# Placing a megakernel's statistics and streamed units by VectorE's other work

## What is computed

```
gn(v):  per group of 2 channels: (v - mean) / sqrt(var + 1e-5)
L0(v):  causal mask (lower triangle), depthwise 6x11 convolution, causal mask again
L1(v):  v + bias[channel, row - column]    (bias from a small three-layer MLP)
x = x + L0(gn(x))
x = x + L1(gn(x))
```

## Time and profile before

| | |
|---|---|
| median of three runs | 2722.15 us (2718.95 to 2722.83) |
| the profiled execution's own time | 2720.33 us |
| its span, first to last instruction | 2718.5 us |
| mean granted TensorE clock | 0.905 |
| VectorE busy | 2307.3 us, 85% |
| TensorE busy | 1986.9 us, 73% |
| ScalarE busy | 1661.5 us, 61% |
| GpSimd busy | 1247.5 us, 46% |
| moved by DMA | 901.17 MB, mean 331 GB/s |

### The profile page before, as it was taken

One profiled execution on the slowest core, in us unless ns is written; L12 is line 12 of the kernel. 1 busy time (PEld: TensorE's weight loads), 2 busy tenths in 40 slices (PEclk: granted clock), 3 DMA queues, 4 the chain that ended last, 5 costly groups with the idle time before them and its releaser, 6 DMA issues. The chain is left out here.

```text
span 2718.5 us, 76785 instructions
## 1 busy us (share of the span) xinstructions
PE 1986.9 (73%) x28880; PEld 1885.9 (69%) x28880; DVE 2307.3 (85%) x4175; ACT 1661.5 (61%) x3051; POOL 1247.5 (46%) x1988
## 2 busy tenths in 40 slices
PE   4299978777787878877678777877768777989500
PEld 0199978777777767877678777777768777879400
DVE  7799988898889988899788998899888996969825
ACT  2177766756576656766567665666657665777521
POOL 1133254545445355544555455454544535655533
PEclk9999999998899989999889988999989998999855
DMA  9756569998899988999799998999889996979899
GB/s 338 274 197 201 192 216 408 357 374 313 325 409 353 367 326 339 399 348 359 293 394 384 353 353 303 405 365 371 323 330 401 354 358 222 351 269 344 303 337 347
DMA packets 316250, 901.17 MB, mean 331 GB/s; under 512 B 42416, under 2 KB 42416, under 8 KB 314000
## 3 DMA queue, kind: packets, MB, share of 16 engines
q1 hardware_dynamic: 199648, 579.79, 58.6%
q10 hardware_dynamic: 116416, 319.37, 30.6%
HBM read 579.50 MB, written 319.68 MB: 331 GB/s over the span
## 5 line engine op out<-in xcount | busy, mean ns | idle before, releaser
L1131 PEld LDWEIGHTS psY<-wsplit,XT 128*128 128x128 f16 x25920 | 1612.4, 102 | 313.7 <-DVE XT L751 116.5
L1131 PE MATMUL psY<-wsplit,XT 128*128 128x168 f16 (+5 forms) x25920 | 1638.1, 223 | 252.5 <-DVE XT L751 217.0
L611 ACT CAST XT<-psT 128x512 f16<-128x512 f32 x720 | 414.5, 576 | 534.6 <-PE psT L1117 316.4
L751 DVE TENSOR_TENSOR XT<-psT,XT 128x512 f16<-128x512 f32 x720 | 493.3, 685 | 191.8 <-ACT XT L611 190.0
L1031 POOL TENSOR_TENSOR xn<-xn,mask 128x512 f32<-128x512 f32 x336 | 440.6, 1311 | 423.4 <-ACT xn L599 364.4
L1117 PE MATMUL psT<-ident,xn 128*128 128x128 f32 x2880 | 486.9, 294 | 177.1 <-POOL xn L1031 136.7
L1066 POOL TENSOR_TENSOR ubuf<-ubuf,bias 128x1024 f32<-128x1024 f32 x184 | 413.5, 2248 | 375.6 <-ACT ubuf L658 375.1
L1057 POOL COPY halo<-XT 128x16 f16<-128x16 f16 x720 | 300.9, 418 | 611.9 <-DVE XT L751 598.9
L779 DVE BATCH_NORM_STATS2 entries<-abuf 128x6 f32<-128x512 f32 x872 | 549.0, 678 | 29.1 <-DMA abuf<-in_x 28.9
L1117 PEld LDWEIGHTS psT<-ident,xn 128*128 128x128 f32 x2880 | 321.8, 148 | 187.9 <-POOL xn L1031 121.6
L599 ACT ACTIVATE xn<-kept_c_band,normp 128x512 f32<-128x512 f32 (+2 forms) x496 | 398.4, 803 | 33.3 <-DMA kept_c_band<-in_x 17.0
(11 more groups left out here) (78 smaller groups left out, 464.1 us busy)
## 6 DMA issues: line engine op xcount, KB each, us to landing
abuf<-in_x SPq DMA_DIRECT2D x436, 512.0 KB, 8.1
out<-ubuf ACTq DMA_DIRECT2D x288, 512.0 KB, 6.2
kept_c_band<-in_x SPq DMA_DIRECT2D x224, 512.0 KB, 8.5
out<-kept_c_band ACTq DMA_DIRECT2D x224, 512.0 KB, 6.9
ubuf<-in_x SPq DMA_DIRECT2D x192, 512.0 KB, 7.1
band<-in_x SPq DMA_DIRECT2D x48, 1024.0 KB, 9.1
out<-band ACTq DMA_DIRECT2D x48, 1024.0 KB, 9.9
ubuf<-out SPq DMA_DIRECT2D x96, 512.0 KB, 8.6
```

The source lines that it names most:

```text
L611: nc.scalar.copy(XT[:, n % NB3, 0, :, 2:P + 2], psT[n % NB3][:, :, :]).then_inc(hi_ready, 1)
L751: nc.vector.tensor_tensor(XT[:, n % NB3, 1, :, 2:P + 2], psT[n % NB3][:, :, :], XT[:, n % NB3, 0, :, 2:P + 2], ALU.subtract).then_inc(lo_r ...
L1131: last = nc.tensor.matmul(psY[m][:, 0:rows, o + lo_c:o + hi_c], XT[:, m, xp, i, 2 - sh:2 - sh + P], wsplit[:, c, wp, K * sh:K * sh + rows, ...
```

## The change

The fixed `U_WEIGHT` goes. A new function `passes()` counts VectorE's other passes at each position: one for the split, one for the eviction, one more on a diagonal tile, two for a kept half, two for early statistics, three for building weights. A position's weight is the sum of these over five positions around it, divided by five times the stage's mean. Both `spread()` calls use this weight, for streamed units and for statistics alike. `U_ON_DVE` is as before.

```
-    U_WEIGHT = lambda n: 1.8 if n < 10 else 1.5 if n > 82 else 1.0
...
+    def passes(do_a, do_b, do_c):
+
+        work = [1.0] * NT
+        for n, (c, b, t) in enumerate(TILES):
+            at = (n + 1) % NT
+            work[at] += 1.0 + is_diag[n]
+        for at in [at for pos in kept_pos.values() for at in pos]:
+            work[at] += 2.0 * do_c
+        for at in EARLY_STATS:
+            work[at] += 2.0 * do_a
+        for at in [W_BUILD[0]] * do_a + [W_BUILD[1]] * do_b:
+            work[at] += 3.0
+        return work
...
+        work = passes(do_a, do_b, do_c)
+        mean = sum(work) / NT
+        lasts = [sum(work[(n + i) % NT] for i in range(-2, 3)) / (5 * mean) for n in range(NT)]
...
-        def spread(count, megabytes, lo, hi, weight):
+        def spread(count, megabytes, lo, hi):
...
-                return max(0.02, level * weight(n) - smooth[n])
+                return max(0.02, level * lasts[n % NT] - smooth[n])
...
-                for at in spread(NU // 2, 1.0, lo, hi, U_WEIGHT if do_a else lambda n: 1.0):
+                for at in spread(NU // 2, 1.0, lo, hi):
...
-            for at in spread(NA, 0.5, A_LO, A_END - 2, lambda n: 1.0):
+            for at in spread(NA, 0.5, A_LO, A_END - 2):
```

## The result

The changed kernel takes 2706.47 us (median of four runs, 2704.06 to 2708.49) against 2722.28 us; the ratio is 0.9944, interval 0.9927 to 0.9961. It is 0.56% faster, clear of noise, where 1.1% was forecast.

The account below looks back on a forecast made before the run. VectorE was taken to set the pace in full stages, with idle time from late loads that stop ScalarE. Full stages -31, stage 1 +7, stage 8 -6.5 and stage 9 +1 took 2720.3 to 2691 us, range 2645 to 2735.

Parts of the forecast that it names:

- The bound: Full stages: VectorE sets the pace in six of twelve stretches; late loads stop ScalarE; keeping 36 us idle would refute it.
- The light stretches of a full stage: Stretches relieved of units, such as 30-38, 74-80 and 81-89: 25.2 us saved in six stretches of stage 4.
- The filled stretches: Stretches given more units, such as 0-14, 47-53 and 61-73: VectorE's added passes show, 12.0 us added per full stage.
- The surcharge: Full stage: costs set against 13.2 us saved: 3 for lock, 4 and 1 for late loads, leaving 5.2, six of them 31.
- The lock: Kept passes behind GpSimd bias adds lose about 1.1 us each; half of six more adds meeting a pass costs 3 us.
- Stage 1: No streamed units, TensorE without a gap; added statistics make VectorE exceed it in places: +7 us (0 to 10).
- Stage 8: Fewer units give 5 us at 30-38, 2 at 39-46, 2.5 from 74; units at 47-49 and before 23 take 3: -6.5.
- The two units taken off VectorE: Two units per stage go to ScalarE and GpSimd; VectorE loses 2 x 1.65 = 3.3 us per full stage.
- A: Rival: transfers are the bound, stalls only move; about 2722 us, or some 2702 with a third less late loads; chance 0.13.
- B: Rival: heavy positions' 20 us all show, light stretches save only 17.6; full stage 2.4 us longer, kernel 2736 us; chance 0.20.
- C: Rival: no late loads, locks cost 1, position 13's stall goes; full stage loses 14 us, kernel 2638 us; chance 0.15.
- D: Rival: positions move but the engines' order hardly does, so there is no change; chance 0.02.

Follow-up runs that it names:

- half the bytes: Each streamed statistics load from the second group on brings half its unit: full stage 317.0 to 306.8 us in the changed kernel, 320.8 to 308.8 in the one before.
- the pair of runs: GpSimd's bias adds cut to 16 columns on both kernels: full stage 313.4 us in the changed kernel, 318.4 in the one before; gap 5.0 in place of 3.8.
- short adds: The changed kernel with GpSimd's bias adds cut to 16 columns: full stage 313.4 us, mean kept pass 1.304 us.
- statistics-only run: The kernel before with only the statistics spread by VectorE's other passes, streamed units as before: 2780.99 us, ratio 1.0233.
- even statistics: The changed kernel with only streamed units spread by VectorE's other passes, statistics spread evenly around them: 2710.41 us, ratio 0.9964.

## Why the prediction missed its size

- **The bound.** Right. VectorE has the most work in a full stage, 283 us, and the idle time is what a plan can change. Late loads stop ScalarE first. But its idle time fell only from 37.2 to 34.3 us a stage, close to the 36 that the prediction had named as a sign of being wrong, and the waits for ScalarE's copy, which were to fall to between 10 and 15 us, rose to 25.2.
- **The light stretches of a full stage.** Right in sign and nearly in size. In stage 4, 30-38 was forecast at 24.8 us and took 23.4, 39-46 at 23.5 and took 24.1, 74-80 at 19.5 and took 20.5, 81-89 at 28.1 and took 27.8 (two of its four units, at 84 and 85, are one position apart and not more, as the prediction had it). The cause I gave for 30-38 was wrong, though: ScalarE was to be the bound with 23.7 us of work. It had 18.8, VectorE 16.4 and TensorE 19.4 of 23.4 us, so no engine filled the stretch.
- **The filled stretches.** 0-14 and 47-53 together were forecast at 97.8 us before any surcharge and took 95.9; 61-73 at 46.7 and 46.4. Here the sum of passes comes out within 2%.
- **The surcharge, 8 us.** It was 318.0 - 307.6 = 10.4 us in stage 4 and 317.0 - 307.6 = 9.4 in the mean, so the full stages gave 22.6 us and not 31. This is one of the two steps that failed. Late loads were priced at 4 us from 47 to 73 and 1 before 29. As means of six stages three stretches were over their forecast by 12.3 us, and the other nine under theirs by 3: 15-22 (24.25 forecast, 28.7 measured), 23-29 (17.7 and 22.3) and 54-60 (25.2 and 28.4), where I had let a wait shrink that in fact went over to ScalarE and from there to all. At 23-29 half the bytes took the whole excess away, so "1 us, between 0 and 4" was a late load priced at under a quarter of its cost. The lock was priced at 3 us; the kept passes of stage 4 lost 28 x (1.610 - 1.467) = 4.0 us more, the streamed ones 13 x 0.37 - 11 x 0.25 = 2.1 less, and the stage 1.2 us by the pair of runs. VectorE's work shows it most at 15-22, 28.2 us where 24.25 was forecast; but neither short adds nor half the bytes (28.8 us) shortened that stretch, so what holds it, when each of the two is gone, stays open.
- **Stage 1.** Forecast +7, measured +6.0.
- **Stage 8.** This is the other step that failed, and the larger: "-6.5", and it was +2.6 us, 9.1 of the 14.9 us by which the sum (-29.5 against -14.6) was off; the full stages are 8.4, the rest goes the other way. I gave 7 us to 30-46 and it was 10.2. I took back 3 us for "three units at 47-49 and more before 23", and 8-22 alone took 10.0. Stage 8 has no statistics: before, VectorE has 16 us of work in the 18.0 us of 8-14 and TensorE 17.3, so that stretch ran at TensorE's pace with hardly a wait to take away. Units bunched at 12-14 and 20-22 bring waits there that it didn't have, 4.25 us of ScalarE's for a load among them. That the places are the cause is shown by the experiment with the old weight in stages 8 and 9, which took both stretches back. How the 10.0 us divide is known only in part, about a third by the bias adds.
- **The two units taken off VectorE.** I counted them in full, 3.3 us a stage. The run that put them back cost 1.4 us a stage.
- **Rivals.** A holds in part: the bytes of half the statistics cost 10 to 12 us a stage in both kernels, and its milder form, 2702 us, came nearer than my 2691. Its strict form fails: 54-73 ran at 393 to 418 GB/s, and the full stages shrank at a mean of 357. B's mechanism is visible in the statistics-only run, 330.0 us a stage: the filled stretches grew by 21.7 us and the relieved ones gave 12.6. C and D didn't occur. That 2706 us lies inside the 2665 to 2710 of the forecast is no proof of it, with two terms off by 8 and 9 us in the same direction.

What stays open: why stage 8 lasts anything from 265.4 to 271.7 us under one and the same plan (the change itself 265 to 267, the versions with other places of the statistics 269 to 272), and what holds ScalarE's copy before position 35, where VectorE waits 2.5 us a stage in the changed kernel and 2.3 with half the bytes. No run was made for either.

## What to carry to other kernels

In a pipeline whose queues run in order, a plan should be costed stage by stage, the partial stages too: a weight that suits the full stage can cost in a stage that another engine paces; here stages 1 and 8 gave back 8.6 of the 22.6 us. The first and the last of the like stages want a look by themselves too, as the 303.4 us of stage 7 with even statistics show. A late load has a place as well as a size; before a unit is given a new position, look what waits stand ahead of its load in the queue. Moving one load alone only made the next ones late here; moving the group together took 2.6 us off a full stage by the profiles, a gain not yet told from none by the whole times. Take a list's parts apart by experiment: here the units' new positions with the statistics left at their old ones brought 1.0%, with both moved 0.4 to 0.6%. And where a gain is some 3 us a stage, lay a profile's reading beside the median of all runs; the one profiled can be 7 us off it.

## What the runs showed of the hardware

A VectorE pass with two SBUF inputs can be stopped even by a GpSimd add that starts with it. This kept pass took 3.46 us against 1.28 alone; it is recorded 0.01 us before an add of 2.36, and ended 1.09 us after it:

```profile
1091.89 3.46 DVE L955 SCALAR_TENSOR_TENSOR kept_c_band<-kept_c_band,outp,bias 128x1024 f32<-128x1024 f32 x1
1091.90 2.36 POOL L1081 TENSOR_TENSOR ubuf<-ubuf,bias 128x1024 f32<-128x1024 f32 x1 [0.98 <-ACT ubuf L673]
```

With adds of 16 columns the mean pass took 1.304 us. The rule of the Trainium skill cited ahead (SBUF — State Buffer, section "SBUF: two separate sides") fits these runs: the pass waits, it isn't slowed in proportion. All the same only part of VectorE's lost time showed in the stage, 3.6 us of 6.6 in the changed kernel and 2.4 of 7.7 in the one before.

One core alone moved 417 and 418 GB/s over stretches of 20 to 27 us. With 13% of a full stage's bytes taken away, by making 58 of its loads half as large, the same instructions in the same order took 3.2 to 3.7% less time a full stage, though the mean DMA rate before had been only 351 to 357 GB/s.
